# Local attention: the cosine product of the rotary step read from PSUM, queries and keys projected into a bank each, and a new order of the turn

## The reference, cut to what matters

```python
h = shift_token(x)
q, k, v = jnp.split(h @ wqkv, 3, axis=-1)        # 8 heads of 64 each
q = l2norm(q) * qs
k = l2norm(k) * ksc
q = q * cos * scale + rotate_half(q) * sin * scale
k = k * cos / scale + rotate_half(k) * sin / scale
# windows of 64 tokens look at themselves and at the window before
sim = where(mask, -max, (8 * q) @ k.T)
o = softmax(sim) @ v
x = x + o @ wo
```

## Time and profile before

| | us |
|---|---|
| median of 3 runs | 2056.72 (2055.81 to 2060.82) |
| the profiled execution, time | 2047.15 |
| the profiled execution, span | 2045.4 |
| first local attention, about | 1092 to 1473 of the span |
| second local attention, about | 1573 to 1944 of the span |
| PE / DVE / ACT / POOL busy over the whole span | 87 / 52 / 73 / 27% |

### The profile page before, as it was taken

One profiled execution on the slowest core, in us unless ns is written; L12 is line 12 of the kernel. 1 busy time (PEld: TensorE's weight loads), 2 busy tenths in 40 slices (PEclk: granted clock), 3 DMA queues, 4 the chain that ended last, 5 costly groups with the idle time before them and its releaser, 6 DMA issues. The chain is left out here.

```text
span 2045.4 us, 68107 instructions
## 1 busy us (share of the span) xinstructions
PE 1782.4 (87%) x28076; PEld 1058.8 (52%) x28076; DVE 1061.3 (52%) x3240; ACT 1483.7 (73%) x2585; POOL 559.8 (27%) x735
## 2 busy tenths in 40 slices
PE   7887899999989999999996787787788777877788
PEld 4674555555545555555543455455433454554533
DVE  4445433333333333333205777877643778787654
ACT  4332899999979999999983767777633577777633
POOL 1004000000000000000005777676101977786300
PEclk9998999999989999999997988988899889998999
DMA  1001211111111111111002100100000001000000
GB/s 55 3 3 44 88 56 57 56 57 57 56 45 57 57 52 49 57 56 40 28 25 75 25 17 16 23 15 10 12 0 10 17 17 24 15 15 18 12 6 36
DMA packets 42329, 69.53 MB, mean 34 GB/s; under 512 B 7376, under 2 KB 33104, under 8 KB 42064
## 3 DMA queue, kind: packets, MB, share of 16 engines
q1 hardware_dynamic: 42064, 65.66, 10.2%
HBM read 21.08 MB, written 2.10 MB: 11 GB/s over the span
## 5 line engine op out<-in xcount | busy, mean ns | idle before, releaser
L653 ACT ACTIVATE x_probs<-x_pss 128x1024 f32<-128x1024 f32 x832 | 806.6, 1021 | 51.2 <-PE x_pss L574 35.3
L588 PE MATMUL x_acc<-x_probs,x_v 128*32 128x256 f32 x6656 | 437.9, 380 | 0.1
L574 PE MATMUL x_pss<-x_qx,x_kx 32*128 32x256 bf16 x9984 | 348.4, 270 | 13.8 <-issue 6.1
L574 PEld LDWEIGHTS x_pss<-x_qx,x_kx 32*128 32x128 bf16 x9984 | 221.4, 93 | 199.4 <-ACT x_probs L653 180.2
L873 POOL TENSOR_TENSOR l_turned_half<-l_raw,l_tabB 128x256 f32<-128x256 f32 x256 | 211.7, 856 | 163.3 <-ACT l_raw L1152 163.3
L588 PEld LDWEIGHTS x_acc<-x_probs,x_v 128*32 128x32 f32 x6656 | 206.6, 110 | 93.5 <-issue 9.3
L1192 ACT ACTIVATE l_prob<-l_sim,l_neg_top,l_inv_norm 128x128 f32<-128x128 f32 x512 | 245.3, 483 | 9.5 <-DVE l_neg_top L1096 9.5
L926 PE MATMUL l_psqk<-w_wqkv,shifted 128*128 128x512 f32 x256 | 155.9, 741 | 85.3 <-ACT l_raw L1152 75.8
L700 DVE COPY x_vnext<-x_psp 128x128 f32<-128x128 f32 (+1 forms) x199 | 59.3, 298 | 315.3 <-PE x_psp L552 312.2
L629 POOL COPY x_zq<-zT 128x256 f32 (+1 forms) x15 | 6.0, 400 | 763.0 <-PE x_psp L559 695.0
L885 POOL TENSOR_TENSOR l_direct<-l_direct,l_turned_half 128x256 f32<-128x256 f32 x256 | 202.0, 820 | 24.3 <-DVE l_direct L1056 20.6
(11 more groups left out here) (166 smaller groups left out, 2670.8 us busy)
## 6 DMA issues: line engine op xcount, KB each, us to landing
x_kx<-x_kp SPq DMA_DIRECT2D x96, 208.0 KB, 2.3
x_cT<-in_context SPq DMA_DIRECT2D x16, 832.0 KB, 4.5
x_qx<-x_qp SPq DMA_DIRECT2D x48, 192.0 KB, 3.4
l_vmid<-l_vt SPq DMA_DIRECT2D x64, 128.0 KB, 2.3
xT<-in_x SPq DMA_DIRECT2D x8, 256.0 KB, 5.2
shifted<-zT SPq DMA_DIRECT2D x32, 64.0 KB, 2.0
out_x<-xT SPq DMA_DIRECT2D x8, 256.0 KB, 2.0
shifted<-zT SPq DMA_DIRECT2D x32, 63.8 KB, 2.0
```

The costliest lines, as they stand in the source:

```text
L574: ins = pe.matmul(pss[bank(k, 2 * p + r // 2)][:, r % 2, e, :], kx[par][rows, g, j * P:(j + 1) * P], qx[par][rows, g, a * S:(a + 1) * S], ...
L588: ins = pe.matmul(acc[32 * r:32 * r + 32, 0:S], v[:, j, g, r, :], probs[SLOT[p]][r // 2][:, r % 2, e, :], start=(u == 0), stop=(u == UNITS ...
L653: act.activation(probs[SLOT[p]][y][:, :, :, :], pss[bank(k, 2 * p + y)][:, :, :, :], ACT.Sigmoid, scale=HD ** -0.5).then_inc(weighed, 1)
```

## The change

All of it is in `local_attention`.
- `psqk` is split into `psq` and `psk`, a bank each, with semaphores of their own. Projection, copy and transposition of queries and of keys become separate steps (`project_q`, `project_k`, `copy_q`, `copy_k`, `flip_q`, `flip_k`) and wait for one bank each.
- `straight_part` becomes `multiply_q` and `multiply_k`: DVE reads the projection from PSUM instead of its copy `raw` in SBUF. They still wait for ACT's copy of the same bank. The next projection into a bank now waits for the product (`straight_q`, `straight_k`), no longer for `raw_ready`.
- ACT's copy into `raw` is two instructions of 128x512 a tile instead of one of 128x1024, and waits for `halved` where it waited for `joined`.
- POOL's steps compute the same in fewer, longer instructions: `turn_halves` 2 of 128x512 (was 4 of 128x256), `join` 1 of 128x1024 (was 4), `scale_keys` 1 of 128x512 (was 2).
- The lists `turn(x)` of PE, DVE, ACT and POOL are in another order. The scores of both blocks of a batch, its block-0 `turn_over` for h = 1 and its `value` for b = 0 move to later places; `flip_q` and `flip_k` for t = 1 now end PE's turn.

```diff
-        psqk = ps("psqk", [P, QK, FD])
+        psq, psk = ps("psq", [P, FH, FD]), ps("psk", [P, FH, FD])
...
-                    pool.wait_ge(straight, 2 * n + t + 1)
-                    for m in range(4):
-                        at = slice(4 * m, 4 * m + 4)
-                        ins = pool.tensor_tensor(direct[r % 2][t][:, at, :], direct[r % 2][t][:, at, :],
-                                                 turned_half[t][:, at, :], ALU.add)
-                    ins.then_inc(joined, 1)
+                    pool.wait_ge(straight_q, 2 * n + t + 1)
+                    pool.wait_ge(straight_k, 2 * n + t + 1)
+                    pool.tensor_tensor(direct[r % 2][t][:, :, :], direct[r % 2][t][:, :, :], turned_half[t][:, :, :],
+                                       ALU.add).then_inc(joined, 1)
...
+                scale_keys(later(x, 1), 0)
+                turn_halves(later(x, 2), 0)
+                join(later(x, 1), 1)
+                scale_keys(later(x, 1), 1)
+                turn_halves(later(x, 2), 1)
+                join(later(x, 2), 0)
...
-                    for m in range(2):
-                        ins = pe.matmul(psqk[:, m * FH:(m + 1) * FH, :], hs[r][:, t * P:(t + 1) * P],
-                                        w["wqkv"][:, m * INNER:(m + 1) * INNER], start=True, stop=True)
-                    ins.then_inc(qk_projected, 1)
+                        pe.wait_ge(straight_k, 2 * n + 1)
+                    pe.matmul(psk[:, :, :], hs[r][:, t * P:(t + 1) * P], w["wqkv"][:, INNER:2 * INNER],
+                              start=True, stop=True).then_inc(k_projected, 1)
...
             def turn(x):
                 project_v(x, 0)
-                project_qk(later(x, 2), 0)
+                score(x, 0)
+                turn_over(later(x, -1), 0, 1)
+                project_k(later(x, 2), 0)
+                project_q(later(x, 2), 0)
+                value(later(x, -1), 0)
                 turn_over(later(x, -1), 1, 0)
+                project_k(later(x, 2), 1)
+                turn_over(later(x, -1), 1, 1)
                 project_v(x, 1)
-                turn_over(later(x, -1), 1, 1)
-                project_qk(later(x, 2), 1, x)
+                project_q(later(x, 2), 1, x)
+                score(x, 1)
                 value(later(x, -1), 1)
-                score(x, 1)
-                flip(later(x, 1), 0)
+                flip_q(later(x, 1), 0)
+                flip_k(later(x, 1), 0)
+                turn_over(x, 0, 0)
                 project_out(later(x, -1))
-                turn_over(x, 0, 0)
-                flip(later(x, 1), 1)
-                turn_over(x, 0, 1)
-                value(x, 0)
-                score(later(x, 1), 0)
+                flip_q(later(x, 1), 1)
+                flip_k(later(x, 1), 1)
...
+            def multiply_q(x, t):
+
+                if exists(x):
+                    n, r, _ = x
+                    dve.wait_ge(raw_q, 2 * n + t + 1)
+                    dve.tensor_tensor(direct[r % 2][t][:, 0:FH, :], psq[:, :, :],
+                                      tabA[:, t, 0, :].unsqueeze(1).broadcast_to([P, FH, FD]),
+                                      ALU.mult).then_inc(straight_q, 1)
...
             def turn(x):
-                norm(later(x, -1), 1, 0)
+                sums(later(x, 1), 1)
                 copy_v(x, 0)
                 mask(x, 0, 0)
+                floor_of(later(x, 1))
+                norm(later(x, -1), 1, 0)
                 norm(later(x, -1), 1, 1)
+                multiply_k(later(x, 2), 0)
+                inverse_norms(later(x, 1))
+                mask(x, 0, 1)
+                multiply_q(later(x, 2), 0)
+                sums(later(x, 2), 0)
                 copy_v(x, 1)
-                mask(x, 0, 1)
-                inverse_norms(later(x, 1))
-                straight_part(later(x, 2), 0)
-                sums(later(x, 2), 0)
                 norm(x, 0, 0)
+                multiply_q(later(x, 2), 1)
+                multiply_k(later(x, 2), 1)
+                mask(x, 1, 0)
+                mask(x, 1, 1)
                 place_keys(later(x, 1), 0)
-                mask(x, 1, 0)
+                add(later(x, -1))
                 norm(x, 0, 1)
-                add(later(x, -1))
-                mask(x, 1, 1)
                 place_keys(later(x, 1), 1)
-                straight_part(later(x, 2), 1)
-                sums(later(x, 2), 1)
-                floor_of(later(x, 2))
...
-            def copy_qk(x, t):
+            def copy_q(x, t):
                 if exists(x):
                     n, _, _ = x
-                    act.wait_ge(qk_projected, 2 * n + t + 1)
-                    at_least(act, joined, 2 * n + t - 1)
-                    act.activation(raw[t][:, :, :], psqk[:, :, :], ACT.Copy).then_inc(raw_ready, 1)
+                    act.wait_ge(q_projected, 2 * n + t + 1)
+                    at_least(act, halved, 4 * n + 2 * t - 2)
+                    act.activation(raw[t][:, 0:FH, :], psq[:, :, :], ACT.Copy).then_inc(raw_q, 1)
+
+            def copy_k(x, t):
+                if exists(x):
...
             def turn(x):
+                place_queries(x, 0)
+                squares(later(x, 1), 1)
+                copy(later(x, -1), 0, 0)
+                exps(later(x, -1), 1, 0)
+                place_queries(x, 1)
+                exps(later(x, -1), 1, 1)
+                copy(later(x, -1), 0, 1)
+                copy_k(later(x, 2), 0)
+                roots(later(x, 1))
+                copy_q(later(x, 2), 0)
+                squares(later(x, 2), 0)
+                exps(x, 0, 0)
+                copy_out(later(x, -1), 0)
+                copy_k(later(x, 2), 1)
                 copy(later(x, -1), 1, 0)
-                roots(later(x, 1))
-                exps(x, 0, 0)
-                copy_qk(later(x, 2), 0)
-                squares(later(x, 2), 0)
                 copy(later(x, -1), 1, 1)
+                copy_q(later(x, 2), 1)
                 exps(x, 0, 1)
-                copy_qk(later(x, 2), 1)
                 copy_out(later(x, -1), 1)
-                place_queries(later(x, 1), 0)
-                copy(x, 0, 0)
-                exps(x, 1, 0)
-                squares(later(x, 2), 1)
-                copy(x, 0, 1)
-                place_queries(later(x, 1), 1)
-                exps(x, 1, 1)
-                copy_out(x, 0)
```

More of the change, by code:

```diff
@@ L868, in turn_halves @@
                     n, r, _ = x
[L869 removed]
+                    pool.wait_ge(raw_q, 2 * n + t + 1)
+                    pool.wait_ge(raw_k, 2 * n + t + 1)
                     for lo, frm in ((0, FD // 2), (FD // 2, 0)):
[L871 to L876 removed]
+                        pool.tensor_tensor(heads(turned_half[t][:, :, lo:lo + FD // 2]),
+                                           heads(raw[t][:, :, frm:frm + FD // 2]),
+                                           table(tabB, t, lo, lo + FD // 2), ALU.mult).then_inc(halved, 1)
             def join(x, t):
@@ L894, in scale_keys @@
                     pool.wait_ge(joined, 2 * n + t + 1)
[L895 to L899, removed]
-            def turn(x):
[L902 to L906, removed]
+                    pool.tensor_tensor(direct[r % 2][t][:, FH:QK, :], direct[r % 2][t][:, FH:QK, :],
+                                       inv_norm[r % 2][:, t, FH:QK].unsqueeze(2).broadcast_to([P, FH, FD]),
+                                       ALU.mult).then_inc(scaled[t], 1)
+            def turn(x):
+                scale_keys(later(x, 1), 0)
[4 more added lines that the diff above has]
+                join(later(x, 2), 0)
             pool.wait_ge(ready, 2)
@@ L932, in project_v, with flip_q, flip_k @@
                     n, r, _ = x
-                    if t == 0:
+                    if t == 1:
+                        pe.wait_ge(v_ready, 2 * n + 1)
+                    elif isinstance(n, int) and n == 1:
+                        pe.wait_ge(v_ready, 2)
+                    else:
                         at_least(pe, added, n - 1)
-                    else:
-                        pe.wait_ge(v_ready, 2 * n + 1)
                     pe.matmul(psvy[:, :], hs[r][:, t * P:(t + 1) * P], w["wqkv"][:, 2 * INNER:3 * INNER],
                               start=True, stop=True).then_inc(v_projected, 1)
-            def flip(x, t):
+            def flip_q(x, t):
+                if exists(x):
+                    n, r, _ = x
+                    pe.wait_ge(joined, 2 * n + t + 1)
+                    if t == 1:
+                        pe.wait_ge(placed_q, 2 * n + 1)
+                    elif exists(later(x, 1)):
+                        pe.wait_ge(straight_q, 2 * n + 4)
+                    else:
+                        pe.wait_ge(placed_q, 2 * n)
+                    for p in range(PH):
+                        ins = pe.transpose(psq[:, 2 * p:2 * p + 2, :].rearrange("p h d -> p (h d)"),
+                                           direct[r % 2][t][:, 2 * p:2 * p + 2, :].rearrange("p h d -> p (h d)"),
```

(8 more changed lines are left out.)

68 lines of the change are left out of this document (44 added, 24 removed).

## The result

The changed kernel takes 1975.03 us (median of 4 runs, 1967.88 to 1978.07) against 2058.77 before; the ratio is 0.9584, 95% interval 0.9548 to 0.9620. The forecast was 1975. That it was met within 1 us is luck: the steady turns gave less than forecast, the ends of the pipeline gave what was counted at nothing, and the profiled execution came out at 1974.57 us where 1965 had been forecast, while the 9.6 us added for the distance from profile to median shrank to 0.5. The profile shows the first two.

The account below looks back on a forecast made before the run. A ring of waits, no engine full, was taken to bound the local attentions. 26 turns x (22.24 - 19.1) = 82 us off the profiled 2047.15 gives 1965, plus 9.6 to the median: 1975 us; 8-in-10 range 1922 to 2040.

Parts of the forecast that it names:

- The bound: Local attentions before: no engine full, a ring of waits across engines sets the 22.24 us turn; PE stalls 2.59 us.
- hand-overs: DVE's idle time in a full-clock turn apart from its waits for the keys: 0.9 us, included in its 16.1 us.
- The product: DVE's cosine product: four from PSUM at 0.68 us replace two of 1.26, +0.2 us a turn; no longer excludes POOL.
- POOL's work: POOL's halves, joins and scales in a turn: 13.5 us taken, bounds 11.3 to 13.5.
- my layout: One turn laid out by hand from the end of the inverse norms, placing POOL, DVE and PE steps to find waits.
- The waits of DVE for POOL: DVE's `neg_top` and `norm` held until a POOL instruction ends: 2.4 us a turn, making 16.1 into 18.5.
- the signs named: Expected in the profile: `neg_top` maximum near 2.8 us, mean 0.5 or more; `norm` mean near 0.8; successor waits within 1.2.
- Rival B: The ring only moves: PE waits for products, placed keys and copies instead; turn 20.6 us, 2015 us; chance 0.20.
- The clock: TensorE's clock still falls, less often than twice a turn, slowing output projection or scores: +0.6 us, giving 19.1.
- The ends of the pipeline: Fill and drain: nothing counted for either; 26 turns save, the 23 measured and 3 beside them.
- From the profile to the median: Whole kernel: the runs' median stands 9.6 us above the profiled execution, so 1965 us becomes 1975.
- Rival C: Slower: DVE blocks on POOL's long instructions, 8 us a turn; decides above 6.1 us; 2106 us; chance 0.11.

Follow-up runs that it names:

- e5: The changed kernel with POOL's join, halves and scale instructions cut to 8 columns, every wait and signal kept: 1862.82 us, ratio 0.9048.
- e4: The changed kernel with both cosine products reading the copy `raw` in SBUF instead of PSUM, same order and waits: 2019.10 us, ratio 0.9841.
- e2: The changed kernel with all of POOL's steps back in short instructions (join 4, halves 4, scale 2): 1903.97 us, ratio 0.9253.
- e6: The changed kernel with two DVE steps swapped, `norm(x, 0, 0)` before `copy_v(x, 1)`: 1891.95 us, ratio 0.9216.
- e1: The changed kernel with only POOL's join cut into 4 instructions of 128x256 again: 1905.21 us, ratio 0.9265.
- e3: The kernel before with POOL's long instructions (join 1, halves 2, scale 1), order and single `psqk` unchanged: 2064.70 us, ratio 1.0064.
- e7: The kernel before, old order and product from `raw`, but with a bank each for queries and keys: 2053.14 us, ratio 0.9970.
- e8: The changed kernel with its two banks guarded as one, by three added PE waits: 1998.76 us, ratio 0.9723.

## Why the prediction was right, step by step

**The bound.** Right in the main: a ring of waits with its stall on PE before, DVE the fullest engine afterwards. e5 puts DVE's own work to the test: 170.12 us busy in 11 turns, 15.5 each, where I had 16.1 with 0.9 of hand-overs in it, so 15.2 without. The hand-overs can't be read from e5, since ACT is busy 16.0 of its 16.4 us a turn (I had 16.3).

**The product.** Right, 0.68 us each. That it stops excluding POOL was told but entered the sum with nothing; e4 shows it to be worth 44 us, the largest of the parts whose taking back cost time. The long POOL instructions are the other way round: taking them back (e2) gains 71 us. Not taken back alone was the new wait of `flip_q`, which now waits for `joined` and no longer for the scaling of the keys.

**POOL's work.** Mis-sized. I took 13.5 us a turn, the upper bound; it is 2 x 2.36 + 4 x 1.24 + 2 x 1.04 = 11.8, near the lower one (1.24 being the start-to-start distance of two halves). With these sizes the join of tile 1 starts 3.5 us after the inverse norms (1.04 + 2 x 1.24), where the sizes of my layout gave 4.0, and the norm at 3.9 comes behind it. Taking POOL too slow hid the long wait.

**The waits of DVE for POOL.** This step failed in size. I had 2.4 us a turn. In 1200 to 1380 us norm's mean is 1.254 us and `neg_top`'s 0.573: 4 x (1.254 - 0.691) + 4 x (0.573 - 0.161) = 3.9 (3.6 over all 24 steady turns). Of the signs named, `neg_top` reached 1.43 us, not 2.8, and a mean of 0.44, while it was norm that reached 2.87 and a mean of 1.23, not 0.8. In my layout the norm comes just before the join; on the chip it comes 0.04 us after it. A layout whose steps carry errors of some tenths cannot decide that race, and e6 shows what hung on it: 3.0 us a turn. The mechanism, one waits for the other's whole instruction, is borne out by e1 to e6: the 2.86 us norm beside the 2.35 us join, the products of e4, and e5 with no wait left. It is the rule that the prediction takes from the Trainium skill, page "SBUF — State Buffer", section "Who interferes with whom"; the trace agrees.

**Rival B.** The turn was 20.2 us, near B's 20.6, and B's path is in part there: `flip_q` waits 2.0 us for `straight_q`, where I had said that no wait would exceed 1.2, and the clock falls behind it in some turns. But the wait begins on DVE, with the norm that lost to the join: e1 and e6 change nothing on PE and gain 70 and 83 us.

**The clock.** Over the 12 steady turns of a layer it stood at 0.94 in both, 0.90 and 0.93 before, and at 1.00 in both layers of e1, e5 and e6. I had 0.6 us a turn for it, and what it costs depends on DVE's waits. The steady turns can be told apart by what waits in them. Where only the norm waits, four turns at 1.00 take 18.4 us and four at 0.91 or 0.92 take 20.1 to 20.3: 1.7 us or more. Where both `neg_top` of block 1 wait too (2.4 us), the turn takes 20.42 at 1.00 and 20.3 to 20.6 in six turns at 0.92: nothing clear, since DVE comes late to its `add` anyway. The waits for POOL and the slow output projection cover each other, they don't add. e1 and e6 take away both: DVE is busy 2.0 and 2.5 us less a turn, the turn is 2.5 and 3.0 shorter.

**The ends of the pipeline.** Counted at nothing, and this error cancelled most of the other. In the profiled executions 72.6 us went away: 531.79 - 485.39 = 46.4 in the 24 steady turns, where I had 3.14 each, 75 (and 82 with two more); 17.6 in the drain (from the last steady `add` to the last one of a layer: 44.28 and 43.91 us before, 35.94 and 34.61 now); 14.9 in the fill (first projection to first `add`: 66.38 and 62.54 before, 58.07 and 55.97 now); less 5.8 by which the first layer starts later. The drain is 34 to 36 us in every kernel of the new order and 43 to 46 in the old (e3, e7), so the order made it, with the waits that it brings. The fill needs the product from PSUM and the separate waits of the banks: both layers together take 128.9 us before, 114.0 now, 127.5 in e4 and 127.8 in e8. The step "I count nothing for either" was the wrong one.

**From the profile to the median.** The profiled execution of the kernel before stood 9.6 us below the median of its runs, and I added this distance. The profiled execution now takes 1974.57 us, 9.6 more than the 1965 I had, and the median stands only 0.5 above it. That the two cancel is chance.

**Rival C**, slower by POOL's long instructions, was the right mechanism at half its price (3.9 us a turn, where it had 8 and 6.1 would have decided). In the old order it costs 0.6% (e3).

## What to carry to other kernels

Where VectorE and GpSimd both work from SBUF, the length of one GpSimd instruction is the price of a lost race for a VectorE instruction with two SBUF inputs: keep these short, or place VectorE's instruction just ahead of the long one (here the two together gained no more than either), and let its other operand come from PSUM where it is there anyway. A layout by hand tells which engine will be full; it does not tell a race that is decided by tenths of a microsecond, so price both outcomes. A wait on one engine can be hidden behind a wait on another: what it costs is read from turns that differ in this one wait. And a software pipeline has a fill and a drain to be laid out like a turn.

## What the runs showed of the hardware

- A VectorE instruction of 0.16 us took up to 1.43, one of 0.69 up to 2.87. In all 67 rows of the changed kernel in which it took over 0.5 or over 0.9 us, its end less its own 0.16 or 0.69 us lies 0.13 to 0.15 us before the end of a GpSimd row. With GpSimd's instructions cut to 8 columns, 0.20 to 0.22 us in the mean (e5), the same rows are 161 to 190 and 691 to 695 ns.
- With one of its two operands in PSUM a VectorE product of 128x512 is 0.68 us beside a busy GpSimd (672 to 693 ns in 128 of them), with both in SBUF 1.15 and 1.64 in the mean (e4).
- One GpSimd sum of 128x1024 takes 2.36 us, four of 128x256 take 2.78.
- The same output projection (8 matmuls of 128x256) took 1.89 us in a turn with a granted clock of 1.00, and 3.47 us in one with 0.92, each time shortly behind 2.0 us in which TensorE stood still. With that wait nearly gone (e1, e6) the clock stood at 1.00 in all steady turns.
